# List sorts whose compared partners lie in SBUF and PSUM, and another order of work around the last attention block

## The chip, the cores and the metric

The kernel is one program on one core of a Trainium2 chip. The metric is the device time of one execution in microseconds (us), the median over several runs. Engines: TensorE (PE), VectorE (DVE), ScalarE (ACT), GpSimd (POOL) and SyncE (SP). Each has its own instruction stream. They meet only through semaphores.

## The reference, cut to what matters

Four graph layers on one graph of 3125 nodes and 100000 edges; each reads the normed node features and adds its result to them.

```python
edge_index = jnp.stack([src, dst])
h = jnp.maximum(_layernorm(x), 0.0)
x = x + _L0_gnn_ref(h, edge_index_t, ...)            # attention, edges in both directions, 4 heads
h = jnp.maximum(_layernorm(x), 0.0)
x = x + _L1_gnn_ref(h, edge_attr_64, ..., edge_index) # two rounds of neighbour means
h = jnp.maximum(_layernorm(x), 0.0)
x = x + _L2_gnn_ref(h, src, dst, ...)                # one round of neighbour differences
h = jnp.maximum(_layernorm(x), 0.0)
x = x + _L3_gnn_ref(h, edge_index, ...)              # attention, 8 heads, then a feed-forward part
```

The two attentions need, for every node, the list of its edges. The kernel sorts the edges by node itself ("list sorts"), once by each end of the edge, for 131072 keys each.

## The kernel before, in words

**First part.** POOL scatters the edges' feature rows to memory: 784 indirect DMAs of 128 rows, `scatter_recs`, line 803. Their data come in turns of eight, loaded and followed up by ACT (`stage`). Behind them stand, in POOL's own order, 50 scatters of the node rows (line 823), two small gathers (line 827), and then the gathers of the first attention.

**List sorts.** Meanwhile DVE sorts two lists, each a tile `SBL` of 128 partitions by 1024 keys (in `oh`). It is a bitonic sort: inside a partition the stages k = 1 to 10, then, for the partners that lie in other partitions, seven rounds in each of which PE transposes the tile into PSUM (`acc`), DVE compares there and PE transposes it back. One stage compares each key with its partner at a distance `1 << q` and writes the smaller and the larger one (`compare`, lines 1383 to 1407). For a block size below 1024 half of the blocks must come out descending, so a stage is four instructions of 256 elements a partition (line 1404); otherwise it is two of 512 (lines 1395 and 1398). `sort_stages` gives the order: 66 stages of the first kind and 87 of the second in each list, 14 turns and 8 multiplications by a sign a partition (line 1412). Every instruction waits for the one before it (semaphore `s_v`). `beside_sort` puts a comparison for another table (line 1357) before each of the first 26 stages of the first list; PE uses it in two products (lines 2209 and 2210), and DVE may be at most two of them ahead.

**After the lists** DVE writes the tables of the attention (lines 1464 to 1520), runs 104 steps of a third sort over the edges (`SB3`), and enters the first attention. The rest of that sort lies in the first eight blocks of the attention.

**First attention.** 54 blocks. For each, POOL issues 32 gathers (line 846) into one of four buffers of `arena`; before block g it waits until DVE has used block g - 4 (`taken0`, semaphore `s_av`). DVE scores, weights and sums the block (`block0`, lines 1638 to 1680).

**Last attention.** 27 blocks, again 32 gathers each (line 846) into four buffers. For a block DVE computes the scores (`begin3`, lines 1589 to 1610, 1959 to 1964), then ACT takes the exponentials. The weighted rows are eight slices for each of four row pairs: DVE writes slices 0 to 3 (`weighted3`, line 1946), ACT slices 4 to 7 (line 1051). PE adds the slices of a pair by eight products with the identity (`sums3`, line 2368). DVE then carries the running state from row to row (`states3`, lines 1925 to 1934). For the blocks before the last, DVE carries rows 4 to 7 of a block in the next block, between its weighted slices. At the end stands an order written by hand (lines 1984 to 2012): the next to last block is called `ahead`, the last `final`. `carried` (line 1701) is the part that takes the states over partitions; it needs five transposes of the last running maxima by PE (lines 2376 and 2377).

**End.** Once the last states are stored (SP, line 757), POOL gathers, corrects and scatters them and gathers the nodes' rows (lines 899 to 904), and the feed-forward part follows.

Of the kernel before, what the change touches and what calls it, by code (L numbers as in the profile page):

```python
# [22 lines left out]
P = 128  # L23
# [90 lines left out]
def build(nc, t, out):  # L114
# [3 lines left out]
    with ctx:  # L118
# [47 lines left out]
        sgn = sb("sgn", [P, 8])  # L166
        pads = sb("pads", [NC, 128])
# [746 lines left out]
        def _(act):  # L914
# [120 lines left out]
            def weights3(a):  # L1035

                act.wait_ge(S["de"], 2 * a.g + 1)
                A.activation(decays3(a), dc[:, a.q], ACT.Exp).then_inc(S["dx"], 1)
                act.wait_ge(S["de"], 2 * a.g + 2)
                if not last_block(a):  # L1040
                    A.activation(weights_of(a), ew[:, a.q].rearrange("p (f k h) -> p f k h", k=8, h=H3)[:, :, 0:8 - VA], ACT.Exp
                                 ).then_inc(S["dx"], 1)
                    act.wait_ge(S["dx"], 3 * a.g + 2)
                A.activation(ew[:, a.q], ew[:, a.q], ACT.Exp).then_inc(S["dx"], 1)
                act.wait_ge(S["dx"], 3 * a.g + 2 + (not last_block(a)))
                for f in range(RH):
# [7 lines left out]
                    if f == 1 and isinstance(a.g, int) and a.g == NB3 - 1:  # L1054
# [32 lines left out]
        def _(v):  # L1087
# [165 lines left out]
            link(V.tensor_scalar(sgn[:, 0:7], sgn[:, 0:7], -2.0, 1.0, ALU.mult, ALU.add))  # L1253
            link(V.tensor_copy(ramp, ramp_i))
# [107 lines left out]
            def overflow_tables():  # L1362

                v.wait_ge(S["ovm"], NC + 1)
                link(V.scalar_tensor_tensor(masks[0][0:1], ramp[0:1], float(TE), acc[0:1, 1536:1536 + NOV], ALU.mult, ALU.add))
# [74 lines left out]

            for l in range(2):
# [10 lines left out]
                at[0] = 0  # L1452
                ordered(SBL, sort_stages(LL))
                assert at[0] == l_at
# [533 lines left out]
            sums = Steps(v, "ds", 24, ahead.g)  # L1988
            sums.k = 12
            for pair in (2, 3):  # L1990
                states3(ahead, sums, pair)
            link(V.tensor_copy(four(resets), rmc[:, 0:P].unsqueeze(1).to_broadcast([P, 4, P])))
            link(V.tensor_tensor(XB[:], Hn[:], lnb[:, 0, :].unsqueeze(1).to_broadcast([P, NC, D]), ALU.add))
            st_ = Steps(v, "dc", 22, final.g)
# [4 lines left out]
            weighted3(final, 1, st_)  # L1999
# [4 lines left out]
            weighted3(final, 2, st_)  # L2004
            sums = Steps(v, "ds", 24, final.g)
            states3(final, sums, 0)
            link(V.tensor_scalar(CMY, bnd[0:H3, 0:P], -1.0, BIG, ALU.add, ALU.mult))
            link(V.tensor_tensor(CMY[:, 1:P], CMY[:, 1:P], Ym[:, 0:P - 1], ALU.add))
            states3(final, sums, 1)
            weighted3(final, 3, st_)  # L2010
            states3(final, sums, 2)
            states3(final, sums, 3)
            assert st_.k == 22 and sums.k == 24
# [102 lines left out]
        def _(pe):  # L2116
# [90 lines left out]
            for j in range(NC + 1):  # L2207
                pe.wait_ge(S["ovk"], j + 1)
                nc.tensor.matmul(acc[0:1, 1536:1536 + NOV], cw[8][:, j:j + 1], masks[j % 2], start=j == 0, stop=j == NC)
                nc.tensor.matmul(pt[0:1, 512:512 + NOV], cw[9][:, j:j + 1], masks[j % 2], start=j == 0, stop=j == NC).then_inc(S["ovm"], 1)  # L2210
# [21 lines left out]
            for l in range(2):  # L2232
                side[0] = 0
                sort_turns(acc, SBL, sort_stages(LL))
                assert side[0] == l_at
# [125 lines left out]
            def sums3(a):  # L2361

                for f in range(RH):
                    pe.wait_ge(S["dvd"], RH * a.g + f + 1)
                    pe.wait_ge(S["dva"], RH * a.g + f + 1)
                    after(pe, S["dpb"], RB * a.g - (6, 0, 2, -4)[f])
                    for k in range(8):
                        last = nc.tensor.matmul(row_bank(2 * f + k // RK), ident[:], V3r[vslot[f]][:, k * 512:(k + 1) * 512],  # L2368
                                                start=k % RK == 0, stop=k % RK == RK - 1)
                    last.then_inc(S["dsm"], 1)  # L2370
            pe.wait_ge(S["asd"], 6)
            quads(pe, NB3 - 1, sums3)
            pe.wait_ge(S["dpb"], RB * (NB3 - 1))
            pe.wait_ge(S["dct"], 1)
            for j in range(4):
                nc.tensor.transpose(pt[:, j * P:(j + 1) * P], MR3[:, j * P:(j + 1) * P], ident[:])
            nc.tensor.transpose(pt[0:H3, 512:512 + P], Y8m, ident[:]).then_inc(S["dcp"], 1)

# [67 lines left out]
```

## Time and profile before

| | |
|---|---|
| median of 3 runs | 5384.65 us (5377.32 to 5385.68) |
| the profiled execution, its own time | 5382.66 us |
| its span | 5380.6 us |
| DVE busy | 3999.8 us (74%) |
| POOL busy | 3577.3 us (66%) |
| PE busy | 2474.7 us (46%) |
| ACT busy | 1275.8 us (24%) |
| granted TensorE clock, mean | 0.628 of full speed |

A time in the rows below is counted from the start of the span. A busy share says how much an engine worked, not whether anybody waited for it: POOL is 66% busy by the records, but a steady 0.3 us lies between two of its indirect DMAs, in which nothing that the profile shows is waited for ("issue"). What ended last is told by the chain of waits, and who was late at one place by the idle time in front of an instruction.

### The profile page before, as it was taken

To read this page: it belongs to the slowest core of one execution; us is meant where nothing else is said; L and a number is where in the kernel's file an instruction comes from. 1 tells how busy PE (TensorE), PEld (TensorE's weight loads), DVE (VectorE), ACT (ScalarE), POOL (GpSimd) and SP (SyncE) were. 2 spreads that over 40 slices of the span, in tenths; PEclk is the share of its full clock that TensorE was granted. 3 is DMA by queue.
4 is the path that set the end of the run, shared out by engine and by line. 5 is a ranking of instruction groups with operands and counts; after the bars stand their busy time and mean duration, and the time that the engine had idled before them with its cause. 6 is when DMAs were issued, how large, how long until landed. Compare 5 with 4: busy or idle time off the path is not lost.

```text
span 5380.6 us, 51142 instructions
## 1 busy us (share of the span) xinstructions
PE 2474.7 (46%) x13030; PEld 1688.7 (31%) x13030; DVE 3999.8 (74%) x7067; ACT 1275.8 (24%) x4464; POOL 3577.3 (66%) x3781
## 2 busy tenths in 40 slices
PE   1697110101222123333333245448983777777775
PEld 0572000101122123323223244437772323333324
DVE  9877888887887578778788787844553777776777
ACT  0000000000000012111111111110002778787771
POOL 1777777777777777777777777740006777777743
PEclk6555555555555555555555555559996888888886
DMA  7212111121222222323323333217771222222212
GB/s 255 59 54 57 49 54 49 47 72 41 54 53 67 61 67 82 84 76 82 84 75 82 84 86 91 83 59 256 248 246 36 88 80 89 88 80 89 88 65 69
DMA packets 391569, 474.83 MB, mean 88 GB/s; under 512 B 216371, under 2 KB 252277, under 8 KB 384166
## 3 DMA queue, kind: packets, MB, share of 16 engines
q1 hardware_dynamic: 135750, 277.58, 15.2%
q0 software_dynamic: 114832, 133.36, 10.8%
q10 hardware_dynamic: 140752, 61.28, 4.0%
q8 instruction: 85, 1.39, 0.1%
q14 instruction: 150, 1.23, 0.1%
HBM read 293.20 MB, written 178.71 MB: 88 GB/s over the span
## 4 chain that ended last, share of the span: by engine, by line
POOL 50%; issue 20%; DVE 16%; PE 9%; DMA 4%; ACT 0%; POOLq 0%; DVEq 0%; ACTq 0%; SPq 0%
POOL arena L846 34%; POOL rec_dram L803 13%; PE acc L2329 3%; DVE OHX L1616 3%; PE pw L2315 2%; DVE arena L1638 1%; DVE arena L1642 1%; DVE V L1658 1%; DVE oh L1626 1%; DVE sc L1643 1%; DMA arena<-tab_dram,jst 1%; DMA V<-in_edge_attr_dram 1%; POOL own_dram L823 1%; DVE oh L1616 1%; DMA rec_dram<-V,rowst 1%
## 5 line engine op out<-in xcount | busy, mean ns | idle before, releaser
L846 POOL DMA_INDIRECT arena<-tab_dram,jst x2592 | 2476.2, 955 | 778.0 <-issue 772.2
L803 POOL DMA_INDIRECT rec_dram<-V,rowst x784 | 837.4, 1068 | 231.9 <-issue 224.0
L2269 PE MATMUL pw<-OHX 128*128 128x128 bf16 x1632 | 209.0, 309 | 737.9 <-DVE OHX L1616 736.7
L2277 PE MATMUL acc<-arena,oh 128*128 128x64 f32 x1952 | 415.0, 412 | 253.3 <-DVE oh L1626 253.3
L2277 PEld LDWEIGHTS acc<-arena,oh 128*128 128x128 f32 x1952 | 405.4, 322 | 267.3 <-issue 267.3
L1051 ACT ACTIVATE arena<-arena,ew 128x64 f32<-128x64 f32 x1728 | 417.8, 333 | 39.7 <-PE acc L2368 39.7
L1051 ACT ACTIVATE OHX<-arena,ew 128x64 f32<-128x64 f32 x1728 | 417.8, 333 | 2.5
L2269 PEld LDWEIGHTS pw<-OHX 128*128 128x128 bf16 x1632 | 155.6, 140 | 789.0 <-DVE OHX L1616 789.0
L2368 PE MATMUL acc<-arena,ident 128*128 128x512 f32 x864 | 382.1, 595 | 29.8 <-ACT arena L1051 22.9
L2368 PE MATMUL acc<-OHX,ident 128*128 128x512 f32 x432 | 261.5, 773 | 291.9 <-ACT OHX L1051 243.7
L1638 DVE TENSOR_TENSOR arena<-arena,pt 128x1024 f32<-128x1024 f32 x108 | 131.8, 1221 | 353.9 <-DMA arena<-tab_dram,jst 351.7
L796 POOL TENSOR_TENSOR pdum<-pdum 128x1 f32<-128x1 f32 x198 | 53.8, 272 | 398.8 <-ACT AS L1017 174.0
L948 ACT COPY V<-arena 128x8 f32 (+1 forms) x98 | 20.0, 205 | 1123.0 <-DMA rec_dram<-V,rowst 1051.4
L2216 PE MATMUL acc<-ident,oh 128*128 128x128 f32 x224 | 55.1, 428 | 487.6 <-DVE vdum L1416 487.6
L978 ACT ACTIVATE arena<-dc 128x476 f32<-128x476 f32 x54 | 57.2, 1059 | 930.3 <-DVE dc L1607 930.3
L1616 DVE TENSOR_TENSOR OHX<-pt,OHX 128x2048 bf16<-128x2048 bf16 x204 | 249.5, 1223 | 6.0
L1404 DVE TENSOR_TENSOR oh<-oh 128x256 f32<-128x256 f32 x528 | 227.7, 431 | 25.0 <-DVE oh L1404 0.5
L2368 PEld LDWEIGHTS acc<-OHX,ident 128*128 128x128 f32 x432 | 106.1, 253 | 446.3 <-issue 446.3
L2368 PEld LDWEIGHTS acc<-arena,ident 128*128 128x128 f32 x864 | 162.2, 190 | 245.4 <-issue 245.4
L1239 DVE TENSOR_TENSOR OHX<-pt,arena 128x364 bf16<-128x364 bf16 x336 | 178.7, 532 | 64.2 <-PE pt L2192 18.5
L1666 DVE TENSOR_REDUCE pt<-V 128x272 f32<-128x1088 f32 x108 | 220.0, 2037 | 3.7
L1826 DVE TENSOR_TENSOR arena<-arena,acc 128x192 f32 x348 | 123.2, 354 | 126.4 <-PE acc L2329 79.7
(588 smaller groups left out, 5894.4 us busy)
## 6 DMA issues: line engine op xcount, KB each, us to landing
arena<-tab_dram,jst POOLq DMA_INDIRECT x2592
arena<-rec_dram SPq DMA_DIRECT2D x122, 288.0 KB, 3.8
mt_dram<-oh ACTq DMA_DIRECT2D x272, 128.0 KB, 1.7
rows_dram<-V SPq DMA_DIRECT2D x27, 1056.0 KB, 4.1
rows_dram<-arena SPq DMA_DIRECT2D x27, 1056.0 KB, 4.3
V<-in_edge_attr_dram ACTq DMA_DIRECT2D x97, 256.0 KB
OHX<-mt_dram SPq DMA_DIRECT2D x39, 512.0 KB, 4.6
oh<-mt_dram SPq DMA_DIRECT2D x39, 512.0 KB, 4.7
```

Source lines behind the costliest of these rows:

```text
L803: gp.indirect_dma_start(rec[:, :], bass.IndirectOffsetOnAxis(ap=rowst[:, q, k:k + 1], axis=0), recst[:, q, k, :], None).then_inc(S[f"scat{ ...
L846: gp.indirect_dma_start(hd.G[:, a.r, j, :], None, table[:, :], row_of(jst[:, a.r, j:j + 1])).then_inc(S[f"rows{a.r}"], 16)
L1051: last = A.activation(V3r[vslot[f]][:, (k * H3 + h) * D:(k * H3 + h + 1) * D], G3[:, a.r, t, 0:D], ACT.Copy, scale=ew[:, a.q, t * H3 + h:t ...
L1239: V.tensor_tensor(paired(o[:, a:a + n]), iota_pairs(n, wide, EP), values[:, k, :].unsqueeze(2).to_broadcast([EP, n, wide // 2, 2]), ALU.is ...
L1404: V.tensor_tensor(o[r], a[r], b[r], op).then_inc(S["v"], 1)
L1616: V.tensor_tensor(paired(mones[c.slot].rearrange("p o t n -> p (o t) n")), iota_pairs(2 * GT, P), SD[:, bass.ds(c.u * (4 * GT), 4 * GT)].r ...
L1638: st(V.tensor_tensor(wv.rearrange("p (f k d) -> p f k d", k=RK, d=D), Ga[:, hf * 16:hf * 16 + 16, 0:D].rearrange("p (f k) d -> p f k d", k ...
L1666: ins = V.tensor_reduce(part.rearrange("p (x f) -> p f x", f=RB), V0[:, :, 2 * k:2 * k + 2].rearrange("p (f k) h e -> p f (h e) k", k=RK), ...
L2269: last = nc.tensor.matmul(unit_bank(c.slot)[:, k // 2 * P:(k // 2 + 1) * P], mones[c.slot][:, 0, k, :], mones[c.slot][:, 1, k, :], start=k ...
L2277: last = nc.tensor.matmul(o, roh[:, c.q, k, :], RG[:, c.r, k, 0:D], start=False, stop=True, skip_group_check=True)
L2329: last = nc.tensor.matmul(group_sum(g), mring[slot][:, g * 4 + k, :], rows_of[:, bass.ds(mine[g * 4 + k] * (3 * D), 3 * D)], start=k == 0, ...
L2368: last = nc.tensor.matmul(row_bank(2 * f + k // RK), ident[:], V3r[vslot[f]][:, k * 512:(k + 1) * 512], start=k % RK == 0, stop=k % RK == ...
```

## The change

**List sorts.** `list_ordered` takes the place of `ordered(SBL, sort_stages(LL))`. The 1024 keys of a partition are held as two halves of 512, `low` in SBUF (`oh`) and `high` in PSUM (`acc`). The halves are parted by that bit of the position that the next stage compares, so each key's partner lies at the same place of the other half. A stage is four instructions of 256 elements: smaller and larger, each for the two values of the bit that follows; those for value 0 go to SBUF, those for value 1 to PSUM. There is a wait only behind the fourth. Descending blocks are had by changing the sign of a part of the keys between the rounds (line 1512 of the new file, and `sgn2`, the product of two neighbouring signs). The last stage in front of a turn (`stage_out`) is two instructions of 512 into one SBUF tile. After a turn DVE waits for both banks of the transpose, copies one half to SBUF and reads the other in PSUM where it lies. A list has 138 stages of four instructions, 15 of two, 14 turns, each with one copy. The helper table's row sums move from `acc` to `accw`, since `acc` is in use. The third sort (`SB3`) is as before.

DVE in the first list, behind its last comparison for the other table, before:

```order
L1404 TENSOR_TENSOR oh<-oh 128x64x4 [waits s_v] x4
L1404 TENSOR_TENSOR oh<-oh 128x128x2 [waits s_v] x4
L1404 TENSOR_TENSOR oh<-oh 128x256 [waits s_v] x4
L1412 TENSOR_SCALAR oh<-oh,sgn 128x1024 [waits s_v]
L1395 TENSOR_TENSOR oh<-oh 128x512 [waits s_v]
L1398 TENSOR_TENSOR oh<-oh 128x512 [waits s_v]
```

and now, at the end of the stages in a partition and the turn behind them:

```order
L1474 TENSOR_TENSOR oh<-oh,acc 128x256 [waits s_v]
L1474 TENSOR_TENSOR acc<-oh,acc 128x256
L1474 TENSOR_TENSOR oh<-oh,acc 128x256
L1474 TENSOR_TENSOR acc<-oh,acc 128x256
L1484 TENSOR_TENSOR oh<-oh,acc 128x512 [waits s_v]
L1484 TENSOR_TENSOR oh<-oh,acc 128x512
L1524 TENSOR_SCALAR oh<-oh,sgn 128x1024 [waits s_v]
L1490 MEMSET vdum 1x1 [waits s_v]
L1496 COPY oh<-acc 128x512 [waits s_stp]
```

Every comparison had both inputs in `oh` (SBUF) and a wait of its own; each now has one input in `oh` and one in `acc` (PSUM), and three of four have no wait.

**Last attention.** In `sums3` PE waits for DVE's slices, adds slices 0 to 3, and only then waits for ACT's. In the order written by hand the scores of the last block (`begin3(final)`) and its first weighted slices lead; the states of the block ahead, the copies for the carry and `XB` (line 1993 before) come between or behind them. PE's five transposes stand inside the last block, behind its second row pair, and ACT's four exponentials for the carry behind its last slices.

DVE at the end of the last attention before, from the last states of the block ahead (`final` begins with line 1589):

```order
L1932 TENSOR_TENSOR arena<-arena,acc 128x512
L1934 TENSOR_TENSOR arena<-arena,rden_ 128x8
L1992 COPY oh<-rmc 128x512
L1993 TENSOR_TENSOR nbr_r<-Hn,lnb 128x1600
L1589 SCALAR_TENSOR_TENSOR arena<-arena,jst 128x8 x8
L1959 TENSOR_TENSOR sc<-arena 128x256
```

and now, where line 1672 is the same step of `final` and line 2029 its first weighted slices:

```order
L1672 SCALAR_TENSOR_TENSOR arena<-arena,jst 128x8 x8
L2042 TENSOR_TENSOR sc<-arena 128x256
...
L2047 TENSOR_REDUCE rden_<-ew 128x64
L2029 TENSOR_TENSOR OHX<-arena,ew 128x1024 x2
L2008 COPY arena<-RUNS 128x4x8
L2012 TENSOR_TENSOR arena<-V,pt 128x512
```

The states of the block ahead (from line 2008 on) now stand behind the last block's scores and its first two weighted pieces.

PE in one row pair of the last block, before and then now:

```order
L2368 MATMUL acc<-OHX,ident 128x512 [waits s_dpb,s_dva,s_dvd]
L2368 MATMUL acc<-OHX,ident 128x512 x7
```

```order
L2451 MATMUL acc<-OHX,ident 128x512 [waits s_dpb,s_dvd]
L2451 MATMUL acc<-OHX,ident 128x512 x3
L2451 MATMUL acc<-OHX,ident 128x512 [waits s_dva]
L2451 MATMUL acc<-OHX,ident 128x512 x3
```

ACT's semaphore `s_dva` is now waited for in the middle of the eight products.

The diff, its core:

```diff
+            def list_ordered():
+                keys, whole, turned_ = SBL[0], SBL[1], acc[:, 0:SWL]
+                lows, highs = [keys[:, 0:512], keys[:, 512:1024]], [acc[:, 1024:1536], acc[:, 1536:2048]]
+                def stage(low, high, bit, following):
+                    beside_sort()
+                    side[0] = 1 - side[0]
+                    to = lows[side[0]], highs[side[0]]
+                    for op, o in ((ALU.min, 0), (ALU.max, 1)):
+                        for w in range(2):
+                            second = part_of_all(turned_, bit, 1, following, w) if high is None else part(high, bit, following, w)
+                            V.tensor_tensor(part(to[w], following, bit, o), part(low, bit, following, w), second, op).then_inc(S["v"], 1)
+                            n[0] += 1
+                    v.wait_ge(S["v"], n[0])
+                    return to
+                def turn_in(bit):
+                    V.memset(vdum[:, 0:1], 0.0).then_inc(S["srt"], 1)
+                    banks[0] += 2
+                    v.wait_ge(S["stp"], banks[0])
...
+                    link(V.tensor_copy(low.rearrange("p (g d) -> p g d", d=1 << bit), half_of_all(turned_, bit, 0)))
+                    for b in range(bit, 0, -1):
+                        low, high = stage(low, None if b == bit else high, b, b - 1)
+                    stage_out(low, None if bit == 0 else high, 0)
...
-                ordered(SBL, sort_stages(LL))
+                list_ordered()
...
-            for pair in (2, 3):
-                states3(ahead, sums, pair)
...
             begin3(final, st_)
             weighted3(final, 0, st_)
+            states3(ahead, carry, 2)
+            weighted3(final, 1, st_)
+            states3(ahead, carry, 3)
...
-                    pe.wait_ge(S["dva"], RH * a.g + f + 1)
                     after(pe, S["dpb"], RB * a.g - (6, 0, 2, -4)[f])
                     for k in range(8):
+                        if k == RK:
+                            pe.wait_ge(S["dva"], RH * a.g + f + 1)
```

## Rows read from the trace of the kernel before

**Rows 1.** The page, the chain that ended last, shares of the span by engine

```profile
POOL 50%; issue 20%; DVE 16%; PE 9%; DMA 4%; ACT 0%; POOLq 0%; DVEq 0%; ACTq 0%; SPq 0%
```

**Rows 2.** Windows, line 803 alone: stretch, length, POOL busy (instructions), clock, DMA share, GB/s

```profile
200.00:400.00 200.00, 149.47 (x156) 0.50 0.20 54
465.00:1103.50 638.50, 486.74 (x443) 0.50 0.19 50
1103.50:1138.00 34.50, 26.64 (x26) 0.50 0.45 149
```

**Rows 3.** Groups of DVE, 200 to 400 us: count, busy us, mean ns, idle before

```profile
L1239 DVE TENSOR_TENSOR OHX<-pt,arena 128x896 bf16<-128x896 bf16 x186 | 116.1, 624 | 27.9 <-DVE OHX L1239 7.9
```

**Rows 4.** Groups of DVE, 465 to 1103.5 us, the two list sorts

```profile
L1404 DVE TENSOR_TENSOR oh<-oh 128x256 f32<-128x256 f32 x528 | 227.7, 431 | 25.0 <-DVE oh L1404 0.5
L1398 DVE TENSOR_TENSOR oh<-oh 128x512 f32<-128x512 f32 x174 | 120.5, 693 | 5.9
...
L1423 DVE COPY oh<-acc 128x512 f32<-128x512 f32 x32 | 22.1, 692 | 22.0 <-PE acc L2216 22.0
...
L1357 DVE TENSOR_SCALAR OHX<-OHX 25x463 f32<-25x463 f32 x26 | 12.6, 486 | 16.0 <-PE pt L2210 15.6
L1412 DVE TENSOR_SCALAR oh<-oh,sgn 128x1024 f32<-128x1024 f32 x16 | 12.0, 753 | 0.7
```

**Rows 5.** Timeline of DVE, instructions with no wait between: start us, us, what

```profile
4899.80 0.69 DVE L1929 TENSOR_TENSOR V<-V,pt 128x512 f32<-128x512 f32 x1
4900.41 0.15 DVE L1930 TENSOR_TENSOR V<-V,pt 128x8 f32<-128x8 f32 x1
```

**Rows 6.** Timeline of DVE, pieces of 256 elements, and the group of line 2074

```profile
465.11 2.55 DVE L1404 TENSOR_TENSOR oh<-oh 128x256 f32<-128x256 f32 x4
...
1132.21 0.29 DVE L1508 TENSOR_SCALAR rmc<-rmc 128x256 f32<-128x256 f32 x1
...
L2074 DVE TENSOR_TENSOR pw<-Hn,pw 128x512 f32<-128x512 f32 x8 | 5.6, 696 | 0.3
```

**Rows 7.** Timeline of POOL: end of the edge scatters, start of blocks 0 and 4

```profile
1211.88 1.11 POOL L796 TENSOR_TENSOR pdum<-pdum 128x1 f32<-128x1 f32 x3
...
1294.41 0.19 POOL L796 TENSOR_TENSOR pdum<-pdum 128x1 f32<-128x1 f32 x1 [5.38 <-DMA jst<-meta_dram]
...
1462.75 0.21 POOL L796 TENSOR_TENSOR pdum<-pdum 128x1 f32<-128x1 f32 x1
```

**Rows 8.** Timeline of DVE, block 0 of the first attention

```profile
1324.32 2.59 DVE L1589 SCALAR_TENSOR_TENSOR pt<-pt,jst,arena 128x64 f32<-128x64 f32 x8
...
1338.89 2.48 DVE L1638 TENSOR_TENSOR arena<-arena,pt 128x1024 f32<-128x1024 f32 x2 [11.99 <-DMA arena<-tab_dram,jst]
...
1368.38 4.11 DVE L1666 TENSOR_REDUCE pt<-V 128x272 f32<-128x1088 f32 x2
```

**Rows 9.** End of the last attention: chain row, then POOL, DVE and ACT

```profile
5144.70 3.65 DMA arena<-tab_dram,jst
...
5184.97 0.94 POOL L846 DMA_INDIRECT arena<-tab_dram,jst  x1 [0.30 <-issue]
...
5200.49 0.42 DVE L1959 TENSOR_TENSOR sc<-arena 128x256 f32<-128x256 f32 x1
...
5205.16 7.74 ACT L1051 ACTIVATE OHX<-arena,ew 128x64 f32<-128x64 f32 x32
```

**Rows 10.** The same stretch: the carry's scan, PE, DVE's last wait, the last store

```profile
5211.36 1.22 DVE L1703 TENSOR_TENSOR_SCAN oh<-oh,pt 128x512 f32<-128x512 f32 x1
...
5213.00 9.93 PE L2368 MATMUL acc<-OHX,ident 128*128 128x512 f32 x16 [2.61 <-issue]
5222.76 7.03 PE L2368 MATMUL acc<-arena,ident 128*128 128x512 f32 x16
...
5244.89 0.69 DVE L1932 TENSOR_TENSOR arena<-arena,acc 128x512 f32<-128x512 f32 x1 [4.56 <-PE acc L2368]
...
5247.53 0.33 SPq L757 DMA_DIRECT2D rows_dram<-arena  x1
```

More of the change, by code:

```diff
@@ L1053, in weights3 @@
                     last.then_inc(S["dva"], 1)
-                    if f == 1 and isinstance(a.g, int) and a.g == NB3 - 1:
+                    if f == RH - 1 and last_block(a):
                         act.wait_ge(S["dcx"], 1)
@@ L1253, in _ @@
             link(V.tensor_scalar(sgn[:, 0:7], sgn[:, 0:7], -2.0, 1.0, ALU.mult, ALU.add))
+            link(V.tensor_tensor(sgn2[:, 0:6], sgn[:, 0:6], sgn[:, 1:7], ALU.mult))
+            link(V.tensor_copy(sgn2[:, 6:7], sgn[:, 6:7]))
             link(V.tensor_copy(ramp, ramp_i))
@@ L1439, in ordered, with part, part_of_all @@
                         compare(bufs, b, c)
+            def part(u, gone, bit, val):
+                if bit < gone:
+                    return u.rearrange("p (a b y d) -> p a b y d", y=2, b=1 << (gone - bit - 1), d=1 << bit)[:, :, :, val, :]
+                return u.rearrange("p (a y b d) -> p a y b d", y=2, b=1 << (bit - gone - 1), d=1 << gone)[:, :, val, :, :]
+            def part_of_all(u, bit, val, other, val_o):
+                high, low = max(bit, other), min(bit, other)
+                x, y = (val, val_o) if bit > other else (val_o, val)
+                return u.rearrange("p (a x b y d) -> p a x b y d", x=2, b=1 << (high - low - 1), y=2, d=1 << low)[:, :, x, :, y, :]
@@ L1987, in _ @@
             final, ahead = [Group(t // 4, t % 4) for t in (NB3 - 1, NB3 - 2)]
[L1988 to L1994 removed]
+            carry, sums, st_ = Steps(v, "ds", 24, ahead.g), Steps(v, "ds", 24, final.g), Steps(v, "dc", 22, final.g)
+            carry.k = 12
             begin3(final, st_)
             weighted3(final, 0, st_)
+            states3(ahead, carry, 2)
+            weighted3(final, 1, st_)
+            states3(ahead, carry, 3)
             link(V.tensor_copy(MR3.rearrange("p (h d) -> p h d", h=H3), heads3.runs(final.q)[:, RB - 1].unsqueeze(2).to_broadcast([P, H3, D])))
             V.tensor_copy(Y8m, heads3.runs(final.q)[:, RB - 1]).then_inc(S["dct"], 1)
[L1999 removed]
+            weighted3(final, 2, st_)
+            link(V.tensor_copy(four(resets), rmc[:, 0:P].unsqueeze(1).to_broadcast([P, 4, P])))
+            link(V.tensor_scalar(CMY, bnd[0:H3, 0:P], -1.0, BIG, ALU.add, ALU.mult))
+            states3(final, sums, 0)
+            weighted3(final, 3, st_)
             v.wait_ge(S["dcp"], 1)
@@ L2003, in _ @@
             V.memset(vdum[:, 3:4], 0.0).then_inc(S["dcx"], 4)
[L2004 to L2007, printed above, removed]
+            states3(final, sums, 1)
             link(V.tensor_tensor(CMY[:, 1:P], CMY[:, 1:P], Ym[:, 0:P - 1], ALU.add))
-            states3(final, sums, 1)
-            weighted3(final, 3, st_)
+            link(V.tensor_tensor(XB[:], Hn[:], lnb[:, 0, :].unsqueeze(1).to_broadcast([P, NC, D]), ALU.add))
             states3(final, sums, 2)
             states3(final, sums, 3)
-            assert st_.k == 22 and sums.k == 24
+            assert st_.k == 22 and sums.k == 24 and carry.k == 24
             V.memset(vdum[:, 0:1], 0.0).then_inc(S["dct"], 1)
@@ L2208, in _ @@
                 pe.wait_ge(S["ovk"], j + 1)
[L2209 removed]
+                nc.tensor.matmul(accw[0:1, 0:NOV], cw[8][:, j:j + 1], masks[j % 2], start=j == 0, stop=j == NC)
                 nc.tensor.matmul(pt[0:1, 512:512 + NOV], cw[9][:, j:j + 1], masks[j % 2], start=j == 0, stop=j == NC).then_inc(S["ovm"], 1)
@@ L2232, in _ @@
             for l in range(2):
-                side[0] = 0
-                sort_turns(acc, SBL, sort_stages(LL))
-                assert side[0] == l_at
+                for _ in range(14):
+                    turns[0] += 1
+                    pe.wait_ge(S["srt"], turns[0])
+                    turn_blocks(acc, SBL[1], SWL // P)
                 turns[0] += 1
@@ L2370, in sums3 @@
                     last.then_inc(S["dsm"], 1)
+                    if f == 1 and last_block(a):
+                        pe.wait_ge(S["dct"], 1)
+                        for j in range(4):
+                            nc.tensor.transpose(pt[:, j * P:(j + 1) * P], MR3[:, j * P:(j + 1) * P], ident[:])
+                        nc.tensor.transpose(pt[0:H3, 512:512 + P], Y8m, ident[:]).then_inc(S["dcp"], 1)
             pe.wait_ge(S["asd"], 6)
             quads(pe, NB3 - 1, sums3)
[L2373 to L2377, printed above, removed]
             sums3(Group((NB3 - 1) // 4, (NB3 - 1) % 4))
```

42 lines of the change are left out of this document (39 added, 3 removed).

## The prediction

> **What bounds the kernel now.** I read the chain of waits first: half of it is POOL, and a fifth is "issue", which is the 0.3 us between two of POOL's indirect DMAs [rows 1]. So POOL's row of indirect DMAs is the spine: 784 edge scatters, 50 node scatters, then 54 blocks of the first attention, and again 27 blocks of the last. DVE is busier (74%) but stands beside it. Next I asked, by windows, how fast POOL goes in each stretch [rows 2]. From 200 to 400 us it does 156 scatters in 200 us, one in 1.282, each 0.958 long. In the list sorts, 465 to 1103.5, it does 443 in 638.5 us, one in 1.441, each 1.099 long. It is the same instruction, with the same 0.3 behind it. What differs is what DVE does: first comparisons with one input in PSUM and one in SBUF [rows 3], then comparisons with both inputs in SBUF [rows 4]. The last thing read is who waits at the junction: POOL ends its scatters at 1211.9 and starts block 0 at 1294.4 [rows 7]; DVE is there at 1324.3 and even stands 12.0 us for rows [rows 8]. So what POOL gains in the sorts reaches the first attention, and from there everything.
>
> **The list sorts, DVE's own time.** Term by term, per list, from the start-to-start times with a wait: a piece of 256 takes (227.7 + 25.0)/528 = 0.479, one of 512 (120.5 + 5.9)/174 = 0.726 [rows 4]. Without a wait the next instruction begins 0.61 behind one that lasts 0.69 [rows 5], so a wait dropped is worth 0.726 - 0.61 = 0.115. A new stage of four pieces, three waits fewer, and each piece taken at 0.425 + 0.035, the usual length and gap of one whose stride is small, is 1.84 - 0.345 = 1.495.
> - 60 narrow stages stay narrow: -0.345 each, -20.7.
> - 6 narrow ones become two of 512: from 1.916 to 1.337, -3.5.
> - 78 wide ones (1.452) become four pieces (1.495): +3.4. 9 stay wide with one wait less: -1.0.
> - Turns: one copy of 0.69 fewer, but now both banks are awaited instead of the first; the second bank was only just ready when the first copy ended (22.0 us of idle over 32 copies [rows 4], 0.69 each, most of it in front of the first). I take 0.
> - Signs: before 8 a list at 0.753 [rows 4]; now 7 of these, 4 pieces of 256 at the start, 8 pairs of 256 and one pair of 512. A piece of 256 is 0.29 from SBUF [rows 6]; from PSUM I take a comparison's 0.425. +8.
>
> That is -14 a list, -28 for two. In the first list PE paces the first 26 stages already (16.0 us idle in front of line 1357 [rows 4]), so 26 x 0.345 = 9 come back. DVE's sorts shrink by some **20 us**, to 618.5. The trace holds no comparison in just this form. Its parts are there: PSUM and SBUF inputs, 0.69 for 512 [rows 5]; a PSUM output, 0.696 [rows 6]. Against it stands one row, 4 pieces in 2.55, or 0.64 each [rows 6]: a stage whose stride is four elements. Bounds for a piece are thus 0.425 and 0.64; I take 0.425, as such strides are rare in the new stages (the first copies and two pieces of a round).
>
> The Trainium skill, page "VectorE: DVE Perf Modes", section "The DRAIN you can't avoid", says that instructions chained without semaphores are no faster than with them, since the pipe empties each time, though it adds that an instruction which is not held starts earlier. By its first statement the 0.115 would be nothing; [rows 5] speak for the second.
>
> **The list sorts, POOL's time.** This is the term that counts. All comparisons now have one SBUF input, like those of [rows 3], so I give POOL the period that it has beside them, 1.282. At 465 us 264 of 784 scatters are done: 784 less the 443 and 26 of [rows 2] and 51 in the 73.9 us from 1138 to 1211.9, which lie beside the third sort (again at 1.441). In 618.5 us come 482, which leaves 38. 26 of them go beside the tables behind the sorts (34.5 us [rows 2]), 12 beside the third sort, which is unchanged, in 17.3 us. The scatters end at 465 + 618.5 + 34.5 + 17.3 = 1135.3 instead of 1211.9: **76.6 us earlier**. If DVE's sorts don't shrink at all, it is 80, since more scatters lie beside them; DVE's length hardly matters here.
>
> The page "SBUF — State Buffer" of the Trainium skill, section "Who interferes with whom", says that a VectorE instruction with two SBUF inputs contends with a GpSimd instruction that reads SBUF; the same section recalls a probe in which `tensor_tensor` did not stall such DMAs. By the first the gain is there, by the second there is none, and the rival below holds it; the 1.099 against 0.958 of [rows 2] agrees with the first.
>
> **Does it reach the end?** POOL's block 0 moves from 1294.4 to 1218. The tables and `s_cb`, which it also needs, are written by the end of the stretch of 34.5 us [rows 2], at 1118 now. DVE comes to its block 0 at 1324.3 - 20 = 1304. POOL may run four blocks ahead: block 4, 168.3 us behind block 0 [rows 7], needs DVE's block 0 weighted, which comes 1368.4 - 1324.3 - 12.0 = 32.1 behind DVE's start [rows 8], at 1336. Block 4 is due at 1386. There are 50 us to spare, so POOL runs on at its own pace, 42 us a block, at which DVE had time to stand and wait before. All 76 go through.
>
> **The end of the last attention.** The last block's rows are there at 5184.97 + 3.7 = 5188.7 [rows 9], but DVE scored them only at 5200.5, behind the states of the block ahead, which waited for PE. Now scoring starts at 5188.7, 11.8 earlier. ACT's slices then start 4.7 later (5205.16 - 5200.49 [rows 9]), at 5193.4, and end at 5201.1, 5208.8, 5216.5 and 5224.1. PE: pair 0 from 5196.6, at the slow level first (9.93 instead of 7.03 [rows 10]), done at 5206.5; pair 1 must wait for the states of the block ahead (5206), done at 5213.4; transposes 5214.7; pair 2 5221.5. DVE, with 2.5 for weighted slices [rows 8], 3.4 for the states of a pair (two times 0.61 and 0.2 and 0.73 and 0.2 [rows 5]) and 5.1 for the carry (a scan of 1.22 [rows 10], three pieces of 512 at 0.73, and small ones): weighted 0, states, weighted 1, states (5206.1), copies and weighted 2 (5210), states of pair 0, weighted 3 (5216.1), the carry, states of pair 1 (5224.7). That frees PE's pair 3, which takes 7.0 to 5231.7; DVE's last two rows take 2.65 (5247.53 - 5244.89 [rows 10]), end 5234.4. The store leaves **13.1 us earlier** than 5247.5. Of it 1.3 come from PE's split wait; in the other 26 blocks the split gains nothing, as POOL's 40.3 us a block (5144.70 to 5184.97 [rows 9]) set the pace. `XB` (1600 elements, 1.8 us at the 1.05 ns an element between pieces of 512 and of 256 [rows 4]) lies in front of DVE's wait for pair 3 and is hidden; uncovered it costs 1.8. If PE starts every pair cold, 3 us go.
>
> **Sum.** 5382.7 (the profiled execution, 2.0 under the median) - 76.6 - 13.1 = 5293, or 5295 against the median. I say **5294**.
>
> **Rivals.**
> - *POOL isn't freed*: the 1.099 came from something else, such as the 50 GB/s of traffic. Against it: the traffic is alike in both stretches (54 and 50 GB/s [rows 2]). Then only the end gains: 5370.
> - *POOL is half freed* (period 1.36; the writes or signs still hold it): 455 scatters in the sorts, end at 1174, 38 us: 5332.
> - *The dropped waits give nothing*: 276 x 0.345 + 30 x 0.115 - 9 = 90 more, DVE's sorts 70 us longer than before. POOL's block 0 comes at 1207, DVE at 1394, its weights at 1426; block 4 starts then instead of at 1462.8. 37 us stay of the first term: 5333.
> - *Slower than before: the pieces that read and write PSUM are long*, and DVE becomes the bound at block 4. The end moves by (1324.3 + d + 32.1) - 1462.8, where d is what DVE's sorts grow; with the 13 of the end it turns into a loss from d = 120, when a piece averages 0.50 instead of 0.37 start to start. At 0.64 long throughout [rows 6], d = 214: 5477. For it: no row has this form. Against it: 0.69 and 0.696 for 512.
>
> **Chances.** Forecast 0.72, its own range 5280 to 5308. Waits worth nothing 0.12, half freed 0.05, not freed 0.07, slower 0.04. Range: 5278 (POOL at 1.26 a scatter in the sorts, the pace of its last attention: 32 in 40.3 us, and 2 or 3 more at the end) to 5342, which takes in all but the last two. A measurement of this kernel tells about 0.2%, 11 us, from no change. Faster 0.93; same 0.03 (half of "not freed"); slower 0.04.
>
> **What would show it.** Line 803 in the sorts at 0.96 and a period near 1.28; its last at about 1134; POOL's block 0 near 1218, and no idle before block 4. The last DVE comparison of the second list near 1083. DVE's pieces at 0.42 with starts 0.34 apart. `begin3` of the last block right behind the last rows, and the last store 13 us nearer to the last gather (49.5 instead of 62.6). It would be wrong if line 803 stays at 1.1 or if POOL stands before block 4.

## The result and the profile after

| | before | after |
|---|---|---|
| median of 4 runs | 5381.71 us (5377.32 to 5385.68) | 5310.3 us (5305.9 to 5310.92) |
| ratio, 95% interval | | 0.9866 [0.9849, 0.9883] |
| span of the profiled execution | 5380.6 us | 5308.5 us |
| DVE / POOL / PE busy | 3999.8 / 3577.3 / 2474.7 us | 3960.8 / 3507.1 / 2501.7 us |

The change gains 71.4 us by the medians and 72.1 by the spans. The time lies in the range, 16 us above the forecast of 5294; the record's two terms, 76.6 and 13.1, add up to 89.7. The chain that ended last is still POOL's (compare [rows 1]):

```profile
POOL 53%; issue 22%; DVE 14%; PE 8%; DMA 2%; ACT 0%; POOLq 0%; DVEq 0%; ACTq 0%; SPq 0%
```

I followed the lead of the changed kernel over the one before through five places: last scatter 66.2 us, block 0 of the first attention 65.8, last gather 70.1, last store 81.6, end of the span 72.1. Against the record that is 10.4 missing at the scatters, 1.6 at the end (11.5 instead of 13.1), and 9.5 lost behind the last store, for which it has no term; 4 us were picked up between.

Windows of line 804 (803 before), same columns as [rows 2]:

```profile
200.00:400.00 200.00, 149.43 (x157) 0.50 0.20 54
465.00:1063.50 598.50, 446.81 (x463) 0.50 0.20 56
1063.50:1098.00 34.50, 26.41 (x25) 0.50 0.44 148
```

In the sorts a scatter comes every 598.5/463 = 1.293 us and takes 0.965. Before it was 1.441 and 1.099 [rows 2].

DVE in the sorts, groups (compare [rows 4]), then its timeline in one turn:

```profile
L1474 DVE TENSOR_TENSOR acc<-oh,acc 128x256 f32<-128x256 f32 x552 | 233.4, 423 | 0.0
L1474 DVE TENSOR_TENSOR oh<-oh,acc 128x256 f32<-128x256 f32 x552 | 230.7, 418 | 9.5
L1496 DVE COPY oh<-acc 128x512 f32<-128x512 f32 x28 | 19.4, 692 | 57.8 <-PE acc L2297 57.8
L1360 DVE TENSOR_SCALAR OHX<-OHX 25x463 f32<-25x463 f32 x26 | 12.8, 494 | 21.4 <-PE pt L2291 21.2
```

```profile
601.54 0.42 DVE L1474 TENSOR_TENSOR oh<-oh,acc 128x256 f32<-128x256 f32 x1
601.88 0.42 DVE L1474 TENSOR_TENSOR acc<-oh,acc 128x256 f32<-128x256 f32 x1
602.21 0.41 DVE L1474 TENSOR_TENSOR oh<-oh,acc 128x256 f32<-128x256 f32 x1
602.54 0.42 DVE L1474 TENSOR_TENSOR acc<-oh,acc 128x256 f32<-128x256 f32 x1
603.00 0.42 DVE L1474 TENSOR_TENSOR oh<-oh,acc 128x256 f32<-128x256 f32 x1
```

Starts lie 0.335 apart without a wait and 0.455 with one; a stage is 1.455. A mixed piece is as long as one in SBUF alone, whichever side it writes to. The second list ends at 1063.5 instead of 1103.6.

POOL, end of the scatters and start of block 0 (compare [rows 7]):

```profile
1145.69 1.10 POOL L797 TENSOR_TENSOR pdum<-pdum 128x1 f32<-128x1 f32 x3
...
1228.61 0.37 POOL L797 TENSOR_TENSOR pdum<-pdum 128x1 f32<-128x1 f32 x1 [5.35 <-DMA jst<-meta_dram]
```

The end of the last attention, POOL, DVE, PE and the store (compare [rows 9] and [rows 10]):

```profile
5114.86 0.94 POOL L847 DMA_INDIRECT arena<-tab_dram,jst  x1 [0.31 <-issue]
5117.34 0.43 DVE L2042 TENSOR_TENSOR sc<-arena 128x256 f32<-128x256 f32 x1 [7.19 <-DMA arena<-tab_dram,jst]
...
5125.18 8.70 PE L2451 MATMUL acc<-OHX,ident 128*128 128x512 f32 x16 [8.70 <-DVE OHX L2029]
...
5153.01 10.12 PE L2451 MATMUL acc<-arena,ident 128*128 128x512 f32 x16 [3.93 <-DVE V L2015]
...
5165.89 0.33 SPq L758 DMA_DIRECT2D rows_dram<-arena  x1
```

From the last gather to the last store it is 51.0 us instead of 62.6. The scores start 2.5 us behind the last gather instead of 15.5. Pair 3 took 10.12, not the 7.0 of the record: PE had stood for 3.9 us in front of it.

Behind the store, PE in the feed-forward part, before and then after:

```profile
5342.12 3.33 PE L2134 MATMUL pt<-ident,Hn 128*64 128x128 f32 x16 [4.60 <-DVE vdum L2103]
5346.11 3.88 PE L2413 MATMUL pw<-arena,F 64*128 64x512 f32 x8 [0.67 <-ACT arena L923]
...
5351.98 3.76 PE L2144 MATMUL acc<-F,arena 128*128 128x64 f32 x32 [0.44 <-ACT arena L923]
```

```profile
5262.35 3.65 PE L2215 MATMUL pt<-ident,Hn 128*64 128x128 f32 x16 [7.79 <-DVE vdum L2184]
5266.67 7.19 PE L2495 MATMUL pw<-arena,F 64*128 64x512 f32 x8 [0.67 <-ACT arena L924]
...
5276.63 7.06 PE L2225 MATMUL acc<-F,arena 128*128 128x64 f32 x32 [0.68 <-ACT arena L924]
```

The same products took twice as long. Windows of PE in this part, after (last columns: granted clock, DMA share, GB/s):

```profile
5222.00:5231.00 9.00, 8.79 (x44) 0.51 0.00 0
5231.00:5241.00 10.00, 7.63 (x46) 0.66 0.00 1
5241.00:5255.00 14.00, 13.56 (x126) 1.00 0.00 1
5255.00:5262.00 7.00, 0.00 (x0) 0.72 0.00 0
5262.00:5293.00 31.00, 28.22 (x89) 0.50 0.00 1
```

PE had reached the high level (2.4 GHz), stood still for 7.8 us, and worked on at the low one (1.2 GHz). The same part before:

```profile
5329.00:5337.50 8.50, 8.50 (x79) 1.00 0.00 0
5342.00:5344.50 2.50, 2.38 (x12) 0.50 0.00 0
5344.50:5346.00 1.50, 0.94 (x6) 0.84 0.05 11
5346.00:5358.00 12.00, 11.17 (x55) 1.00 0.00 1
```

There PE stood for 4.6 us and also came out of the pause at the low level, but was back at the high one before the first product, which started 4.0 us behind the pause. The two products cost 6.6 us, and 1.0 more goes in the transposes and products around them. The other 1.9 lie ahead: PE's combining products ran at the low level, ACT's copies and exponentials behind them came later, and DVE waited 2.88 instead of 0.58 us for ACT. Together that is the 9.5.

### The profile page after: what moved, and what is told of

It reads as the page before. It is cut to its first block, busy times and chain, and to the rows that moved or that the text cites. A ratio compares the mean times of both kernels' runs of the same rounds, so it can differ in the third digit from the quotient of the medians.

```text
span 5308.5 us, 51276 instructions
## 1 busy us (share of the span) xinstructions
PE 2501.7 (47%) x13030; PEld 1704.5 (32%) x13030; DVE 3960.8 (75%) x7371; ACT 1273.0 (24%) x4464; POOL 3507.1 (66%) x3781
## 3 DMA queue, kind: packets, MB, share of 16 engines
q1 hardware_dynamic: 135750, 277.58, 15.5%
## 4 chain that ended last, share of the span: by engine, by line
POOL 53%; issue 22%; DVE 14%; PE 8%; DMA 2%; ACT 0%; POOLq 0%; DVEq 0%; ACTq 0%; SPq 0%
POOL arena L847 37%; POOL rec_dram L804 12%; PE acc L2411 3%; DVE OHX L1699 3%; PE pw L2397 3%; POOL own_dram L824 1%; DVE arena L1721 1%; DVE V L1741 1%; DVE arena L1725 1%; DVE oh L1709 1%; DVE sc L1726 1%; POOL arena L877 1%; DMA arena<-tab_dram,jst 1%; DVE oh L1699 1%; POOL pdum L797 1%
## 5 line engine op out<-in xcount | busy, mean ns | idle before, releaser
L804 POOL DMA_INDIRECT rec_dram<-V,rowst x784 | 776.1, 990 | 233.2 <-issue 230.0
L1474 DVE TENSOR_TENSOR oh<-oh,acc 128x256 f32<-128x256 f32 x552 | 230.7, 418 | 9.5
L1474 DVE TENSOR_TENSOR acc<-oh,acc 128x256 f32<-128x256 f32 x552 | 233.4, 423 | 0.0
```

The lines of the kernel that those rows point to most:

```text
L804: gp.indirect_dma_start(rec[:, :], bass.IndirectOffsetOnAxis(ap=rowst[:, q, k:k + 1], axis=0), recst[:, q, k, :], None).then_inc(S[f"scat{ ...
L1474: V.tensor_tensor(part(to[w], following, bit, o), part(low, bit, following, w), second, op).then_inc(S["v"], 1)
```

## Experiments

All ratios are to the kernel before on the same chip. The experiments ran on three chips, on which the kernel before has medians of 5382.89 (`high_in_sbuf`, `wait_each`, `sort_only`, `tail_busy`), 5378.49 (`after_again`, `keep_warm`, `third_parted`, `no_split`) and 5380.35 (`before_dropped`, `end_only`, `pair3_busy`, `both_and_warm`). I was after three questions: what freed POOL, what the dropped waits are worth, and whose the 9.5 us are.

**What freed POOL: the place of the input, or DVE's new rhythm?** First the upper halves back in SBUF:

```diff
+        HX = sb("HX", [P, 1024])
-                ... [acc[:, 1024:1536], acc[:, 1536:2048]]
+                ... [HX[:, 0:512], HX[:, 512:1024]]
```

> The changed kernel with one thing put back: the upper halves of the lists (`highs`) lie in a new SBUF tile instead of in `acc`, so that nearly all comparisons again have both inputs in SBUF. Their number, their order and the dropped waits stay. Theory A (the place of the second input frees POOL): line 804 goes back to 1.10 in the sorts, one scatter in 1.44 us, the last scatter to about 1212 instead of 1145.7, block 0 to 1294, and the time to 5376. Rival (the new rhythm of DVE, three of four pieces without a wait, frees it): line 804 stays at 0.96 and the time at 5310. The pieces of DVE should take 0.42 to 0.48 in either case.

Measured: 5358.69 us (5376 expected), 0.9956 [0.9939, 0.9973], of which the new end, kept here, is 12. The window of its scatters and its largest DVE group:

```profile
465.00:1062.00 597.00, 454.86 (x424) 0.50 0.19 51
...
L1475 DVE TENSOR_TENSOR oh<-oh,HX 128x256 f32<-128x256 f32 x500 | 211.1, 422 | 8.5
```

DVE's pieces did not change (422 ns), yet POOL fell back to 1.073 a scatter and a period of 1.408; block 0 came at 1280.7, 51.4 later than in the changed kernel. So the place frees POOL. It is not the whole: 14 us of the 65.8 stay with both inputs in SBUF, since 1.408 is not 1.441; dropping the waits does as much by itself (below). A look at single scatters of the changed kernel fits: of 399 between 545 and 1062 us, 6 were above 1.05, five beside sign passes of line 1524 and one beside that of line 1514, all with one input, from SBUF to SBUF; the other seven of the twelve passes of line 1524 held no scatter above 1.05. Before, between 545 and 1100, it was 280 of 381. The Trainium skill, page "SBUF — State Buffer", section "Who interferes with whom", gives the rule (two SBUF inputs contend with a GpSimd instruction that reads SBUF), and this pair of runs agrees; the section's recollection that `tensor_tensor` did not stall such DMAs does not hold here.

Then the places kept and the waits put back:

```diff
                             V.tensor_tensor(part(to[w], ...), part(low, ...), second, op).then_inc(S["v"], 1)
                             n[0] += 1
+                            v.wait_ge(S["v"], n[0])
```

(and the same in `stage_out`).

> The changed kernel with a wait behind every comparison of the list sorts again; places and order stay. Each of some 850 dropped waits costs 0.115, less 9 us in the first list, where PE sets the pace: the second list ends at about 1154 instead of 1063.5. Theory A: POOL does not care, line 804 stays at 0.96, and as no scatter is left for the slow stretch, the last one even comes 8 us earlier, at 1137. DVE's block 0 starts at about 1374 instead of 1284 and frees its buffer at 1406; POOL's block 4 would be due at 1391, so it waits some 15 us and starts 7 later than now: 5317. Rival (the rhythm frees POOL): line 804 at 1.1, last scatter near 1212, 5376 or more.

Measured: 5374.22 us, 0.9983 [0.9974, 0.9993]. Its scatters, then POOL in front of its fourth block (block 3) and DVE's start of block 0:

```profile
465.00:1140.00 675.00, 501.33 (x519) 0.50 0.20 55
...
1411.98 0.19 POOL L797 TENSOR_TENSOR pdum<-pdum 128x1 f32<-128x1 f32 x1 [56.66 <-DMA jst<-meta_dram]
...
1404.91 2.26 DVE L1674 SCALAR_TENSOR_TENSOR pt<-pt,jst,arena 128x64 f32<-128x64 f32 x7
```

The half on POOL came as expected: 0.966 and 1.301, block 0 at 1219.4. The total did not: 57 us late. Two numbers of mine were wrong. A dropped wait is worth 0.145, not 0.115 (a piece averages 0.473 against 0.364 with three of four waits gone, so a stage 0.435), and DVE comes to block 0 120.7 us later, not 90. And POOL isn't held by block 4 and DVE's weights, but by block 3: SP loads that block's indices (`meta3`) only behind the memset with which DVE enters block 0, and they are there 7.1 us later. This wait of 56.7 ate the gain. So the place alone does not pay in this kernel: with the waits the whole change is worth 9 us, less than its new end (12, below). SP's wait is in the code too: `load_meta` for block 3 stands behind `S["cb"]`, which that memset raises.

The dropped waits in the old form, both inputs in SBUF:

```diff
                             V.tensor_tensor(o[r], a[r], b[r], op).then_inc(S["v"], 1)
                             n[0] += 1
-                            v.wait_ge(S["v"], n[0])
+                            if bufs is not SBL or (k, r) == (1, 1):
+                                v.wait_ge(S["v"], n[0])
```

> The kernel before with one edit: in the list sorts only the last comparison of a stage is waited for; both inputs stay in SBUF, the form of the stages too. By the price that the run with a wait behind each piece gave (0.145 each), a list is 66 x 0.435 + 87 x 0.145 = 41 shorter, both some 71 with PE pacing the first stages: the second list ends near 1032 instead of 1103.6. Theory A (the place of the second input counts): POOL still takes some 1.41 us a scatter, as with the upper halves in SBUF, its last near 1197 instead of 1211, and DVE's 71 us buy nothing more: 5368. Rival (a shorter DVE sort is itself the gain): POOL ends its scatters 40 us or more earlier, 5340 or less.

Measured: 5359.88 us, 0.9962 [0.9948, 0.9976]. The second list ended at 1032.6, the last scatter started at 1196.9, one every 567/404 = 1.403 us, all as expected. Block 0 came at 1278.4 (16.7 earlier), and at the last gather the lead was 20.8: so the time is 8 us lower than expected. DVE, 71 us ahead, runs more of the third sort before POOL's first blocks, where it slows nobody's gathers; that reading was not tested by itself, and 4 of these us came between block 0 and the last gather, where alike traces differ by up to 12. Side by side: dropped waits alone are worth 20 us, the place alone (with the waits, and less the new end) nothing, and both together, in the run with the sorts alone, 55. The place frees POOL, and the dropped waits bring DVE to block 0 in time for it.

**Does the rule carry on?** The front of the third sort had both inputs in SBUF still. It was given the same form, up to the end of its third round:

```diff
-            at[0] = 0
-            ordered(SB3, edge_sort[0:SORT_FRONT])
+            list_ordered(SB3, pw[:, 0:SWL], 4)
+            V.memset(vdum[:, 0:1], 0.0).then_inc(S["srt"], 1)
+            at[0] = 1
```

> The changed kernel, and the stages of the third sort that lie before the first attention (to the end of its third round) written in the same parted form: one input in SBUF, one in PSUM, three of four comparisons without a wait. Theory A (place of the second input): the scatters and the node scatters beside it take 1.29 instead of 1.44 us each; in the 130 us from 1098 to block 0 that is some 83 instructions by 0.15, 12.5 us: block 0 at 1216, the time 5298. DVE's part of it shortens by 17. Rival (the gain of the sorts came from something else in them, such as what ACT and SP do meanwhile): POOL keeps its 1.44 there and the time is 5310.

Measured: 5289.87 us, 0.9835 [0.9817, 0.9853]. POOL from 1098 to 1200 us, in the changed kernel and then in this one:

```profile
L824 POOL DMA_INDIRECT own_dram<-arena,rst_u x37 | 41.7, 1128 | 12.5 <-issue 12.5
L804 POOL DMA_INDIRECT rec_dram<-V,rowst x34 | 38.7, 1138 | 9.8 <-issue 9.5 <-ACT rowst L950 0.3
```

```profile
L824 POOL DMA_INDIRECT own_dram<-arena,rst_u x46 | 44.4, 965 | 15.7 <-issue 15.7
L804 POOL DMA_INDIRECT rec_dram<-V,rowst x33 | 31.8, 964 | 9.5 <-issue 9.2 <-ACT rowst L950 0.3
```

Block 0 came at 1215.07 (1216 expected), 14.2 earlier. This form drops waits as well, so the run doesn't part the two. The time was expected at 5298. In the traces the span is 25.8 shorter; of that 2.8 lie between the last gather and the last store (pair 3 took 7.10 instead of 10.12) and 9.6 behind the store, where the clock was high. The medians differ by 20.4; the four times spread from 5280.61 to 5295.49, and only one of them, 5284.84, has a trace.

**The end.** The list sorts alone, and the new end alone, on the kernel before (each takes the other's lines of the diff out):

> The kernel before with the list sorts alone changed; the last attention and PE's order are as before. Up to the last gather as the changed kernel (5114.9). From there to the last store 62.5 us instead of 51.0. The two theories differ in what is behind the store, where the changed kernel lost 9.5 us (142.6 to the end of the span instead of 133.1). If that loss belongs to the new order of the end (TensorE's clock in the last part follows what PE did before), it goes away: 5312, so that the whole change of the end is worth 2 us. If it came with the sorts, it stays: 5322.

> The kernel before with only the new order of the end (DVE's order, PE's split wait, ACT's exponentials). Up to the last gather as before (5185). From it to the last store 49.7, the mean of seven traces that have the new end, instead of 62.6: 12.9 earlier, 5369. Rival (the old states order hid part of it, or the end's gain is only there with the new sorts): 5375 or more.

Measured: sorts alone 5327.85 (5322 or 5312 expected), 0.9893 [0.9876, 0.9909]; its last gather came 10.5 later than in the changed kernel, on code that but for PE's split wait is the same up to there. End alone 5368.74, 0.9982 [0.9972, 0.9991]. From the last gather to the last store it was 61.6 with the old end and 49.7 with the new. The end is worth 12 us in either setting. Then the split wait taken back:

```diff
                     pe.wait_ge(S["dvd"], RH * a.g + f + 1)
+                    pe.wait_ge(S["dva"], RH * a.g + f + 1)
...
-                        if k == RK:
-                            pe.wait_ge(S["dva"], RH * a.g + f + 1)
```

> The changed kernel, but PE again waits for ACT's slices before the first product of a row pair, not in the middle. The record puts 1.3 us on this, all in the last block; the other 26 are paced by POOL. Expected: last gather to last store 52.3 instead of 51.0, time 5311.5. Rival: ACT ends its slices 4 us or more behind DVE in each pair, pairs 0 and 3 begin later, and the end loses 4 to 5 us: 5315.

Measured: 5309.95, 0.9875 [0.9859, 0.9892]. Its trace has 53.7 from gather to store (52.3 expected), 4 above the 49.7 that is usual with the split, and 5.5 above the 48.2 of the two traces with the split in which pair 3 took 7.10 without fillers, as it did here. Then it has 133.0 to the end of the span with the high clock. The time thus shows nothing, though the place shows 4 to 5.5 us; one trace is too little to hold that number.

**Behind the store.** The first try filled both of PE's pauses:

```diff
+            busy(105)
+            pe.wait_ge(S["deg"], 8 * 16)
+            busy(22)
             for c in range(NC + 1):
...
+            busy(52, pu)
             pe.wait_ge(S["ev"], 12 + 1)
```

> The changed kernel with TensorE kept busy by transposes of the identity that nobody reads: 127 of them in the 27 us in which it waits for the nodes' rows, and 52 before the feed-forward part, in free PSUM banks. Theory: the 9.5 us lost behind the last store are the clock level (the product of line 2495 took 7.19 at 1.2 GHz instead of 3.88, line 2225 7.06 instead of 3.76). At the high level throughout, they come back and the time is 5301 or a little less. Rival (something else than the clock, or the idle transposes only get in the way): 5310 or up to 5 us more.

> The changed kernel once more, beside the others on the same chip, since parts that are alike in two kernels differed by up to 9 us at the last gather between two traces. Expected: 5310, the last gather between 5112 and 5126. Whether TensorE is at 2.4 or 1.2 GHz in the feed-forward part (line 2495 at 3.88 or 7.19) is what this trace adds: if it is chance, it may be either.

> The changed kernel with 52 transposes of the identity, read by nobody, into a free bank in front of the feed-forward part, where TensorE otherwise stands still for 7.8 us; nothing in the earlier gap. Theory (the clock falls in that pause): line 2495 takes 3.88, line 2225 3.76, and from the last store to the end it is 135.2 instead of 142.6, so 5303. Rival: the clock falls anyway, or the 5.9 us that the run with both fillings gained behind its last store were chance: 5310.

> The changed kernel with 28 transposes of the identity, read by nobody, between PE's pair 2 and pair 3 of the last block, where it stands 3.9 us; nothing else. Theory (the pause lets the clock fall): pair 3 takes 7.1 instead of 10.1 and the last store leaves 3 us nearer to the last gather, 46.7 instead of 49.7. Rival (the clock falls anyway, or the fillers hold pair 3 up): 49.7 or up to 2 more.

| | time | ratio, interval | last gather | gather to store | store to end | product of 512 columns |
|---|---|---|---|---|---|---|
| after | 5310.3 | 0.9866 [0.9849, 0.9883] | 5114.9 | 51.0 | 142.6 | 7.19 |
| the same again | 5311.21 | 0.9875 [0.9858, 0.9891] | 5115.8 | 49.7 | 145.3 | 7.19 |
| both pauses filled | 5310.6 | 0.9866 [0.985, 0.9882] | 5123.8 | 49.7 | 136.7 | 3.88 |
| 52 ahead of feed-forward | 5304.05 | 0.986 [0.9844, 0.9877] | 5122.8 | 49.8 | 135.5 | 3.88 |
| 28 ahead of pair 3 | 5304.64 | 0.9857 [0.984, 0.9873] | 5123.0 | 48.0 | 134.4 | 3.88 |
| third sort | 5289.87 | 0.9835 [0.9817, 0.9853] | 5101.5 | 48.2 | 133.0 | 3.88 |
| split taken back | 5309.95 | 0.9875 [0.9859, 0.9892] | 5112.8 | 53.7 | 133.0 | 3.88 |
| sorts alone | 5327.85 | 0.9893 [0.9876, 0.9909] | 5125.4 | 61.6 | 141.5 | 7.19 |
| end alone | 5368.74 | 0.9982 [0.9972, 0.9991] | 5187.2 | 49.7 | 140.6 | 7.19 |
| before | 5381.71 | | 5185.0 | 62.6 | 133.1 | 3.88 |

The last column is the first product of the feed-forward part (line 2495 of the new file). PE in front of it with 52 idle transposes, and in front of pair 3 with 28:

```profile
5264.83 5.85 PE L2240 MATMUL pw<-ident 128*128 128x128 f32 x52
...
5273.56 3.88 PE L2501 MATMUL pw<-arena,F 64*128 64x512 f32 x8 [0.67 <-ACT arena L924]
```

```profile
5157.08 3.22 PE L2240 MATMUL acc<-ident 128*128 128x128 f32 x28
5161.16 7.11 PE L2456 MATMUL acc<-arena,ident 128*128 128x512 f32 x16 [0.86 <-DVE V L2015]
```

With the fillers the product is at 3.88 and pair 3 at 7.11. For pair 3 that shows less than it seems: in nine traces without fillers there it took 10.1 twice, 8.8 four times and 7.10 three times. The 28 transposes made the way from gather to store 48.0, not the 46.7 expected: 1.7 below the usual 49.7, and no less than the 48.2 of the traces with 7.10 and no filler. Behind the store, every trace with the product at 7.19 has 140.6 to 145.3 and every one at 3.88 has 133.0 to 137.0 (the other four traces fit: 145.3 at 7.19, and 135.3, 135.4 and 137.0 at 3.88). So the loss is the clock. Whose is it? Not the sorts' and not the end's: either alone shows the low level, and the third sort, the split taken back and the filler ahead of pair 3, which touch nothing behind the store, show the high one. PE's pause ahead of the feed-forward part was 7.3 to 7.8 us in three traces without the 52 transposes and 4.6 to 5.4 in the eight others, and in all eleven the clock right behind it was 0.50. What differs is whether it was back at 1.00 by the product: not in the three with the longer pause, nor in the run again and the one with the upper halves in SBUF (both 4.6); in the other six it was (five at 4.6, one at 5.4). Whether it comes back in time, these runs don't let one foresee; that fillers keep 1.00 throughout, the three traces with 52 transposes show. The fillers in the earlier pause bought nothing: the combining products behind them ran at the low level for most of their length all the same, and the time stayed at 5310.6 where 5301 was expected. 52 transposes gain 7 us here (7.2 against the run again, by the medians), though the trace of `keep_warm` itself arrives 7 us later at the last gather. Stretches that are alike in code differ that much: from block 0 to the last gather the traces have 3882.1 to 3894.2 (the run with the waits back apart).

**All that helped, together** (third sort, 28 and 52 transposes):

> The changed kernel with three additions: the front of the third sort in the parted form, 28 idle transposes in front of PE's pair 3 of the last block and 52 in front of the feed-forward part. Expected: block 0 at 1215, last gather to last store 46.7, from there to the end 133 to 135.5 in every execution: 5284, some 5 below the kernel with the third sort alone (5289.9), and with less spread. Rival: the idle transposes buy nothing, 5290.

Measured: 5286.32 us (5283.74 to 5288.89; 5284 expected), 0.9827 [0.9811, 0.9843]. It beats both kernels. From gather to store its trace has 48.2 instead of the 46.7 expected, as the third sort alone had. Over the third sort alone (5280.61 to 5295.49) the fillers bring 3.5 us, less than the two samples, which come from two chips, tell apart, and a narrower spread.

## Why the prediction was right, and where its sizes were off

**The spine and the term that counts** were right. POOL was freed by the input's place, and the lead at block 0 went through the whole first attention. Forecast 76.6, measured 66.2. Of the missing 10.4, 5.0 are the period (463 scatters at 1.293 instead of 1.282). Some 3 come from where the scatters lie: 463 instead of 482 were done in the sorts, mostly since DVE ended these 20 us sooner than forecast, and one behind them takes some 0.15 more. The rest, 2 to 3, lies in the stretches behind the sorts (25 scatters instead of 26 in the 34.5 us of the tables) and isn't parted further.

**DVE's sorts** shrank by 40, not 20. The failed step is the price of a narrow stage: "1.84 - 0.345 = 1.495". It took off three waits at 0.115 from a stage at 1.84, but a stage was 1.916 by the same rows (1.892 in the new form with its waits), the waits are worth 0.145, and what is left is 1.455. That is 0.116 more for each of 60 stages and 0.04 for each of 78 wide ones, some 10 us a list. The Trainium skill, page "VectorE: DVE Perf Modes", section "The DRAIN you can't avoid", has a chain without semaphores take as long as one with them, and adds that a next instruction that is not held starts earlier. The run with the waits back, 0.145 us a piece, agrees with the addition and not with the first. The bound of 0.64 for a piece did not come true.

**"DVE's length hardly matters here"** held for the scatters (the last one starts at 1134.7 with DVE 121 us later at block 0, at 1144.5 without) and failed for the kernel. **"There are 50 us to spare"** rested on block 4 and on DVE's weights; the gate is block 3 and DVE's entry into block 0. In the changed kernel block 3 starts at 1357.7 and its indices could be there at 1284.3 + 7.1 = 1291.4, so 66 us were to spare and the sum did not suffer. The rival "the dropped waits give nothing" did: it was priced at 5333 and measures 5374, outside the range. Its chance of 0.12 was given to a loss of nearly all the gain.

**The end**: 13.1 forecast, 11.5 in the trace, 62.0 - 49.7 = 12.3 over three traces with the old end and eight with the new. "49.5 instead of 62.6" is the mean of these eight to 0.2. In the profiled trace pair 3 ran at the low level, 3 us, which the record named as a risk; a scoring that started 1.2 earlier than forecast gave a part back. The split wait may be worth more than 1.3, and XB was hidden.

**Behind the last store** the record has no term. It took the part as unchanged, and the work is. But it contains two products, 7.6 us on the chain, whose length doubles with the clock, and the trace of before had the short one. These 9.5 us and the 10.4 of the scatters are what the forecast had too much; the 4.3 picked up between block 0 and the last gather lie within what alike traces differ by.

## What to carry to other kernels

Where one engine issues indirect DMAs back to back and another computes beside it, ask of each computing instruction how many inputs it reads from SBUF: here, with one in PSUM, an issue took 0.965 us instead of 1.06 to 1.1, at no cost to the computing engine. Before calling slack enough, find the last link of the gate (here a load of indices that SP starts when DVE enters a block), and put the wait back by experiment to learn what dropping it is worth. The part at the end, with short products on the chain, had two lengths here (133.0 to 137.0 and 140.6 to 145.3); compare such a part apart from the total. With 52 idle transposes in the pause ahead of it, it was the short one in all three traces that had them.

## What the runs showed of the hardware that I had not expected

- An indirect DMA's issue on POOL takes 0.965 beside comparisons with one SBUF and one PSUM input and 1.059 to 1.1 beside such with two SBUF inputs (1.059 in the old form with dropped waits, 1.073 in the new form), though half of the mixed pieces write SBUF. Beside one-input passes from SBUF to SBUF (lines 1514 and 1524) single issues took up to 1.45, but seven of the twelve passes of line 1524 slowed none by so much.
- A comparison of 256 elements takes 0.42 with both inputs in SBUF (the run with the upper halves there) and with one in PSUM, whichever side it writes to; the next without a wait starts 0.335 behind.
- After a pause of 4.6 us ahead of the feed-forward part PE went on at 1.2 GHz in all seven traces with it; in five it was back at 2.4 GHz by the first product, 4.0 to 4.3 us later, and in two it stayed low, in kernels that differ only far ahead of it. After 3.7 to 4.0 us ahead of pair 3, pair 3 took from 7.10 to 10.17.
